# Sums over a 64-step chunk: one 128-row product per head pair, or two 64-row products on two row tiles, with new issue orders around them

## The reference, cut to what matters

```python
alpha = jax.nn.sigmoid(jax.nn.silu(x @ Wad.T + bad) @ Wau.T + bau)
alpha = jnp.clip(alpha, ALPHA_MIN, 1.0)
...
def chunk_step(S, inp):
    qc, kc, vc, ac, bc = inp
    O_inter = jnp.einsum('bcd,bde->bce', qc, S)
    cl = jnp.cumsum(jnp.log(jnp.maximum(ac, 1e-07)), axis=1)
    cum = jnp.exp(cl[:, :, None, :] - cl[:, None, :, :]) * mask[None, :, :, None]
    A = jnp.einsum('bid,bijd,bjd->bij', qc, cum, kc * bc)
    O = O_inter + jnp.einsum('bij,bje->bie', A, vc)
```

## Time and profile before

| what | us |
|---|---|
| median of 3 runs (2667.97 to 2676.7) | 2672.06 |
| the profiled execution, its own time | 2680.18 |
| its span, first to last instruction | 2677.7 |
| stage three | about 960 to 2678 of the span |
| a round: from 977.4 (first F of lane a) to 2593.6 (last of lane b) lie 15 rounds and the 39.7 from lane a to b | 105.1 |
| PE busy over the span | 2339.2 (87%) |
| ACT, DVE busy | 1622.6 (61%), 1615.5 (60%) |
| granted TensorE clock, mean; from 1100 to 2600 | 0.974; 1.00 |

### The profile page before, as it was taken

How to read it: one execution, slowest core, us unless ns; L and a number is a source line. 1 busy time by engine, 2 the same in 40 slices (tenths; PEclk the granted TensorE clock), 3 DMA queues, 4 the chain that set the end, 5 groups by cost and what they waited for, 6 DMA issues and landing times.

```text
span 2677.7 us, 93035 instructions
## 1 busy us (share of the span) xinstructions
PE 2339.2 (87%) x41378; PEld 1733.9 (65%) x41378; DVE 1615.5 (60%) x3692; ACT 1622.6 (61%) x3788; POOL 295.4 (11%) x396
## 2 busy tenths in 40 slices
PE   3888888888888559999999999999999999999997
PEld 2666566666666337767667677676676676776765
DVE  3666766676667555655665655555555656565564
ACT  2767666766676335656656656656566566566663
POOL 0001110111010001011001001100110011011100
PEclk8999999999999779999999999999999999999998
DMA  3000000000000100000000000000000000000000
GB/s 110 8 9 7 10 8 9 9 8 8 9 9 8 31 25 7 6 8 7 7 9 7 7 8 7 7 7 6 9 7 7 9 6 7 8 7 6 8 6 4
DMA packets 55338, 29.76 MB, mean 11 GB/s; under 512 B 24225, under 2 KB 53217, under 8 KB 54945
## 3 DMA queue, kind: packets, MB, share of 16 engines
q1 hardware_dynamic: 50624, 21.90, 3.0%
q10 hardware_dynamic: 4320, 1.97, 0.3%
HBM read 18.60 MB, written 5.24 MB: 9 GB/s over the span
## 4 chain that ended last, share of the span: by engine, by line
PE 38%; DVE 13%; ACT 11%; issue 2%; DMA 0%; SPq 0%; DVEq 0%
PE bank L1120 5%; PE bank L1187 2%; PE bank L1317 2%; ACT PT L1372 2%; DVE h L1520 2%; DVE zels L451 2%; ACT zels L1372 2%; DVE m L449 2%; PE bank L1250 2%; PE bank L1150 1%; PE bank L356 1%; PE bank L1310 1%; DVE h L1633 1%; PE bank L1160 1%; ACT zels L1392 1%
## 5 line engine op out<-in xcount | busy, mean ns | idle before, releaser
L1030 POOL TENSOR_TENSOR PT<-zels,unit 128x512 f32<-128x512 f32 x160 | 203.7, 1273 | 1469.5 <-ACT zels L1372 1282.0
L356 PE MATMUL bank<-w_gate,ident 128*128 128x128 f32 (+3 forms) x1024 | 316.0, 397 | 14.4 <-DVE mx L876 14.4
L425 ACT ACTIVATE zels<-zels 128x512 f32<-128x512 f32 x384 | 237.8, 632 | 105.4 <-DVE zels L451 105.0
L451 DVE TENSOR_TENSOR zels<-bank,m 128x512 f32<-128x512 f32 x384 | 265.6, 692 | 13.3
L449 DVE TENSOR_REDUCE m<-bank 128x4 f32<-128x512 f32 x384 | 262.1, 683 | 18.2 <-PE bank L370 10.4
L391 PE MATMUL bank<-ident,zels 128*128 128x128 f32 x1536 | 223.0, 282 | 17.7 <-ACT zels L425 13.2
L1372 ACT ACTIVATE zels<-bank 128x512 f32<-128x512 f32 (+1 forms) x256 | 142.6, 573 | 151.8 <-PE bank L1219 76.1
L391 PEld LDWEIGHTS bank<-ident,zels 128*128 128x128 f32 x1536 | 170.9, 143 | 54.8 <-ACT zels L425 38.6
L1372 ACT ACTIVATE PT<-bank 128x512 f32<-128x512 f32 x256 | 148.0, 598 | 92.5 <-PE bank L1293 50.4
L428 ACT ACTIVATE PT<-bank 128x512 f32<-128x512 f32 x384 | 202.3, 597 | 2.4 <-PE bank L391 2.3
L356 PEld LDWEIGHTS bank<-w_gate,ident 128*128 128x128 f32 x1024 | 159.8, 194 | 57.6 <-issue 33.7
(11 more groups left out here) (292 smaller groups left out, 5025.2 us busy)
## 6 DMA issues: line engine op xcount, KB each, us to landing
ctxT<-in_ctxT_dram SPq DMA_DIRECT2D x64, 48.0 KB, 1.8
x_after_cross_attention<-x SPq DMA_DIRECT2D x32, 64.0 KB, 1.5
h<-x_after_cross_attention SPq DMA_DIRECT2D x8, 256.0 KB, 2.8
xin<-x_after_cross_attention SPq DMA_DIRECT2D x32, 64.0 KB, 1.8
out_dram<-xn SPq DMA_DIRECT2D x32, 64.0 KB, 1.6
x<-in_xT_dram ACTq DMA_DIRECT2D x30, 64.0 KB, 1.8
input_integers<-xq SPq DMA_DIRECT2D x8, 128.0 KB, 2.0
xq<-input_integers SPq DMA_DIRECT2D x32, 32.0 KB, 1.8
```

The lines of the kernel that those rows point to most:

```text
L356: mm(bank[:, 0:cols], ident[:, :], w_gate[:, :, :].rearrange("p a b -> p (a b)")[:, 0:cols], start=True, stop=True)
L425: act.activation(n.zels[:, u, :], n.zels[:, u, :], ACT.Exp, scale=ATT_SCALE).then_inc(ph.act[s], ph.AC.step(s, f"{t}P{u}"))
L451: dve.tensor_tensor(n.zels[:, u, :].rearrange("p (h k) -> p h k", h=HU), scores, top.unsqueeze(2).broadcast_to([P, HU, P]), ALU.subtract). ...
L1030: pool.tensor_tensor(n.TI[:, k % 2, :, :], (n.PT0, n.PT1)[k % 2][:, :, 1, :], unit[:, :].unsqueeze(1).broadcast_to([P, NP, DK]), ALU.add)\
```

## The change

Stage F now takes two products for a pair: chunk 0 with rows 0 to 63 of the logarithms as weights and the upper left 64x64 block of `since` as the moving operand, chunk 1 with rows 64 to 127 and the lower right block. The first goes to bank 2, the second to bank 3. There are 16 products of 64 rows and 64 moving columns in place of 8 of 128 and 128. One semaphore step `cum` after the last product replaces `cum0` and `cum1`. ScalarE still takes four exponentials of 128x512; each now reads one chunk's bank and writes 64 of every 128 columns. The four order strings are new, and so is the fill: 13 units for each lane in both, at other stages. POOL's string starts lane b at stage 44 rather than 18.

```diff
-            "pe": (35, "100101001010001101011011010111010101000110010000101101110101110011101010110100110101",
...
+            "pe": (35, "100100100110101001010101100110010110001001101100101101110110110011101010110110010110",
...
-            "pool": (18, "111101101011001001110111000110001001101110010101110001000101010011110110101101000100",
...
+            "pool": (44, "000001101010101001110010111111010101010110001001000110111111000000000101101101011100",
...
-        CWARM = {"h": 0, "conv": 2, "alpha": 3, "F": 0, "norm1": 0, "bc": 0, "fc": 4, "pj": 0, "yq": 1, "Wo1": 0,
-                 "lna": 1, "lnav": 0, "lngv": 1, "lny": 0, "lnyv": 0, "lnf": 0, "lnfv": 1,
+        CWARM = {"h": 1, "conv": 0, "alpha": 0, "F": 1, "norm1": 0, "bc": 3, "fc": 0, "pj": 0, "yq": 3, "Wo1": 0,
+                 "lna": 0, "lnav": 1, "lngv": 0, "lny": 0, "lnyv": 0, "lnf": 3, "lnfv": 1,
...
                         for i in range(2):
                             act_did(f"aL{i}")
                             for p in range(4 * i, 4 * i + 4):
-                                last = mm(pair_out(p, 2), n.B[:, p, :], since[:, :], start=True, stop=True)
-                            last.then_inc(pc.pe[s], pc.PE.step(s, f"cum{i}"))
+                                for c, (lo, hi) in enumerate(halves):
+                                    last = mm(b[2 + c][:, p * DK:(p + 1) * DK], n.B[lo:hi, p, :], since[lo:hi, lo:hi], start=True, stop=True)
+                        last.then_inc(pc.pe[s], pc.PE.step(s, "cum"))
...
                         for i in range(2):
-                            pe_did(f"cum{i}")
-                            f(quad(n.Fp, i), b[2 + i][:, :], ACT.Exp, f"Fp{i}", scale=-1.0)
-                            f(quad(n.Fm, i), b[2 + i][:, :], ACT.Exp, f"Fm{i}")
+                            chunk = slice(DK * i, DK * (i + 1))
+                            sums = b[2 + i][:, :].rearrange("p (a t) -> p a t", t=DK)
+                            pe_did("cum")
+                            f(n.Fp[:, :, chunk], sums, ACT.Exp, f"Fp{i}", scale=-1.0)
+                            f(n.Fm[:, :, chunk], sums, ACT.Exp, f"Fm{i}")
```

More of the change, by code:

```diff
@@ L498, in decoder @@
         pc = Part(sem, "c",
-            [*norm_pe("a"), "mid", "al0", "al1", "gb", "cum0", "cum1", "Q0", "Q1", "K0", "K1", "ssq", "V1", "M", "cdT", "cds", "V0",
+            [*norm_pe("a"), "mid", "al0", "al1", "gb", "cum", "Q0", "Q1", "K0", "K1", "ssq", "V1", "M", "cdT", "cds", "V0",
              "T0", *[x for name in SOLVE for x in ((name, "KmT") if name == f"W{LEVELS - 2}" else (name,))], "S", "Oi", "O0", "O1", "mo", "bc", y_pe[0], "Wo1", "lngv",
@@ L998, in decoder @@
         CSLOTS = slots_of(CSTAGES, {
-            "pe": (35, "100101001010001101011011010111010101000110010000101101110101110011101010110100110101",
[L1000 to L1004, removed]
-            "pool": (18, "111101101011001001110111000110001001101110010101110001000101010011110110101101000100",
-                   "10011100110011100100010001100000110101"),
+            "pe": (35, "100100100110101001010101100110010110001001101100101101110110110011101010110110010110",
+                   "11010101010110100101000111000100101000"),
+            "act": (35, "001010011001010101000111010110010001101110001100101110111011011001011101011010011011",
+                   "01101001110001100110101010000001001100"),
+            "dve": (36, "010000101110010010110000111101010010010111001010111011010110011110101001101100111010",
+                   "10101011000011101010011100010000010101"),
+            "pool": (44, "000001101010101001110010111111010101010110001001000110111111000000000101101101011100",
+                   "10100100101011101101000101110110010011"),
         }, TAILS)
         C_LOADS = 4
-        CWARM = {"h": 0, "conv": 2, "alpha": 3, "F": 0, "norm1": 0, "bc": 0, "fc": 4, "pj": 0, "yq": 1, "Wo1": 0,
-                 "lna": 1, "lnav": 0, "lngv": 1, "lny": 0, "lnyv": 0, "lnf": 0, "lnfv": 1,
+        CWARM = {"h": 1, "conv": 0, "alpha": 0, "F": 1, "norm1": 0, "bc": 3, "fc": 0, "pj": 0, "yq": 3, "Wo1": 0,
+                 "lna": 0, "lnav": 1, "lngv": 0, "lny": 0, "lnyv": 0, "lnf": 3, "lnfv": 1,
                  "y": {"S": 0, "P": 0, "OT": 0, "AT": 0}}
```

## The result

The changed kernel takes 2753.3 us (median of 4 runs, 2741.4 to 2758.8), the kernel before beside it 2670.1 us: a ratio of 1.030, 95% interval 1.027 to 1.033. It is slower by 83 us, and outside the range. The profiled execution took 2741.4 us, the least of the four, with a span of 2739.0 against 2677.7.

The account below looks back on a forecast made before the run. TensorE's order was taken to set the pace, with 7.8 us idle in a 105.1 us round. Products, step and fill at 0, orders -1 us and a shorter last record -1 took 2672.06 to 2670 us; range 2640 to 2699.

Parts of the forecast that it names:

- Part 1: F's products on PE: 16 overlapping pairs take 1.8 us, as 16 records before, since weight loads set the pace; 0.
- a shorter last record: F's last record on PE was said to be shorter, taking 1 us more off the total time.
- Part 2: One step for both banks: exponentials start 1.0 us later but are covered; cost 0, up to 0.3 a lane.
- Part 3: Fill on PE: 13 units a lane before and after, 0.21 us each; sum unchanged, worth something only inside a wait.
- the walk: Hand trace of one round, 1641.37 to 1746.51, under the new orders; 22 waits, good to about 1 us a round.
- Part 4: The new orders: leads and lags at eight places sum to -0.05 us a round, -1 us over 16 rounds.
- leads at `S` and in `O`: Lane b's `S` starts 0.6 us ahead, and the end of `O` comes 0.8 us ahead, in the new order.
- The clock: TensorE's granted clock was forecast to stay at 1.00 from 1200 to 2500 us.
- The slower rival: Lane b's norm behind lane a's convolution delays `yq`; 2688 us, told by over 2.5 us before L1334; 0.26 with small waits.
- the rule of the Trainium skill: Up to 2x for F's products, as the halved-F rival: 14 to 29 us less, 2643 to 2657 us; chance 0.10.

Follow-up runs that it names:

- before, new fill: The kernel before with only the changed kernel's table of fill, orders and gate sums as before; 2712.2 us, ratio 1.014.
- before, less fill: The kernel before with 6 of its 26 units of fill a round taken away; 2674.5 us, ratio 1.001.
- new orders, old F: The changed kernel's order strings and fill with the kernel before's whole products and two steps; 2733.7 us, ratio 1.018.
- after, fill behind: The changed kernel with 10 more units of fill a round, ahead of F and so behind the waits; 2773.3 us, ratio 1.037.
- after, old fill: The changed kernel with the fill table of the kernel before; 2784.1 us, ratio 1.043.
- after, norm first: The changed kernel with lane b's output projection and norm turns ahead of lane a's convolution on VectorE and ScalarE; 2848.9 us, ratio 1.067.
- before, one stretch new: The kernel before with the changed kernel's turns from lane a's first norm to its gate sums, on three engines; 2779.1 us, ratio 1.040.
- after, stretch back: The changed kernel with the kernel before's fill and its turns from lane a's first norm to its gate sums; 2763.7 us, ratio 1.035.
- gate sums alone: The kernel before with only the new F lines; first run 2683.7 and 2692.2 us (two other executions disturbed), second run 2685.9 us, ratio 1.006.
- one step alone: The kernel before with the gate sums' two semaphore steps made one, products whole; 2680.3 us, ratio 1.003.
- the waits filled: The changed kernel with lane b fill added, 6 units before the query (L1334), 4 before the convolution's second half (L1148); 2708.1 us, ratio 1.012.

## Why the prediction was wrong

The sum of what was measured, from 2753.3 us down: filling two waits takes away 45 us (the clock), halving the fill, from 36 units to 18 that stand in waits, takes away 24, the old gate sums change nothing that can be told (+3.7), and 13 are left to the new turns (2683.9 and 2687.6 against 2670.6 and 2674.9 beside them). The shares go by this order of steps: taken away first, the old gate sums gave some 20 us, with the scatter told above.

- **Part 1** was right: nothing won, nothing lost in the products' time (1.93 us from F's first product to the next stage's in the changed kernel at full clock, against 2.09 and 1.98 before). The 1 us taken off for a shorter last record isn't there: it is 272 ns long and was 275. What it left out is the clock: in the old orders a wait before the 64-row products is followed by falls, and the same wait before whole ones is not.
- **Part 2** was mis-sized at its edge. Cost 0 was taken; measured in the old orders was a wait of 0.28 us a round, near the end of the bound (0.3), and in the new ones nothing.
- **Part 3 is the step that failed first.** "The sum is unchanged" counts the units and not their places. The same 13 units moved alone cost 39 us. The 5 units ahead of `conv` and `alpha` covered waits, as the walk itself says of lane b, where it has 0.8 and 1.2 us come out instead of 0.1, but the price of fill where it had been hiding a wait was not carried through both lanes.
- **Part 4** found the places of the waits, and nearly their sizes: 1.26 before L1334 (1.55 forecast), 1.0 (1.2) and 0.5 (0.8) for lane b's `alpha` and `conv`, 0.8 (0.85) before L1183, 0.5 (0.65) for `fc`, and the six that were to go went. It came out level, though, where the measured round is 2.0 us longer at full clock, and PE idle for 1.5 us more. A part of the miss is a wait that it did not have, 0.7 us before L1133. Another may be the round that it was held against, one of 105.1 us, where undisturbed rounds of the same trace take 103.84: the round walked has a wait of 0.8 us before L1234 that they lack. How much of the 1.2 us between them the walk carried into the new order can't be told, so this share stays open.
- The **leads at `S` and in `O`** (0.6 and 0.8 us) were priced as if PE set the pace there. In the old orders a wait of 0.7 us removed before L1293 was worth 0.15 us, and 1.28 us of fill 0.23.
- **The clock is the largest miss, 45 us.** The text has 1.00 from 1200 to 2500; it was 0.98, with 68 us at half. The slower rival had the right wait, the right cause (lane b's norm behind lane a's convolution) and the right consequence ("a lower clock behind it"), but put its point at 2.5 us and priced no fall. The wait was 1.26 us, half of that, and was followed by a fall in 6 of 15 rounds. Nothing in the trace of before excluded it: its three falls stand behind waits of 0.9, 1.9 and 1.6 us (the last two for nothing that the profile names), which a reading by a window of 1300 us at clock 1.00 does not show.

On the rule of the Trainium skill ("TensorEngine Tiling (Array Packing)", section "Theoretical Speedup"), up to 2x for a dimension up to 64: the trace shows no gain over whole products, since 762 records of 64x64 take the 50.9 us of 400 whole ones. What the two row tiles give is that the 64-row records overlap: 32 of them take 2.00 us, where one after another at 0.116 us each they would take 3.7, an estimate from the earlier trace rows. The prediction read the rule as a gain from splitting a whole product, which is not what these rows show. The Trainium skill, "TensorE: Matmul & The Clock Gate", section "LDWEIGHTS (loading the stationary operand)", says that a load's time goes by its columns and not by the contraction; the trace agrees: with half the rows and still 128 columns, a load takes 199 ns, and took 191.

What stays open is why one wait of a given length is followed by a fall and another is not (below), and which of the new turns make the 13 us at full clock. No run changed GpSimd's order by itself.

## What to carry to other kernels

Where an engine is busy for 93% and its waits are short, what counts is not how many waits a new order removes but which long ones it makes, what stands in them and what behind them. Put a price on a fall of the clock behind each of TensorE's longest waits (45 us here, for two waits of 1.3 and 1.0 us a round), and put filler work into those waits first. Cost filler by its place and its lane, never by the sum of its units. And take the baseline of a walk from the rounds that are undisturbed (here 103.84 us, where the mean is 105.0).

## What the runs showed of the hardware

In a stage where TensorE is busy for over 90% of the time, its granted clock falls from 2.4 to 1.2 GHz soon after idle waits of 0.6 to 2.7 us, and not after each wait of a given length. In this table a fall counts for a wait if it begins within the wait or within 8 us of its end. All of them begin by 2.9 us after the end; those before L370 in "before, less fill" begin 0.0 to 0.3 us after it. The table is worked out from the waits and the clock records of each trace; it has the waits of this length from 1010 us to the end of the last round.

| kernel | wait of PE | times | followed by a fall |
|---|---|---|---|
| all | 0.7 us, before L409 | 15 each | 0 |
| before, new fill | 0.7, before L1148, lane a (0.7 and 0.8 shortly ahead) | 15 | 4 |
| before, new fill | 1.0, before L1148, lane b | 12 | 0 |
| before | 1.1, before L370 | 15 | 0 |
| before, less fill | 1.1, before L370 | 15 | 4 |
| new orders, old F | 1.3, before L1333 | 15 | 12 |
| after | 1.3, before L1334 | 15 | 6 |
| after | 1.0, before L1148, lane b | 14 | 2 |
| after, fill behind | 1.3, before L1334 | 15 | 11 |
| after, old fill | 1.9, before L1334 | 15 | 8 |
| after, norm first | 2.7, before L1148, lane a | 15 | 15 |
| after, norm first | 1.0, before L1148, lane b | 13 | 10 |
| before, one stretch new | 1.9, before L1333 | 15 | 9 |
| before, one stretch new | 2.2, before L391 | 15 | 2 |
| after, stretch back | 1.1, before L1161 (64-row products) | 15 | 15 |
| gate sums alone, first and second run | 0.6, before L1161 (64-row products) | 15 each | 3, 5 |
| before; one step alone | 0.6, before L1160 (whole products) | 15 each | 0 |

Length alone does not decide. What PE does behind the wait has a hand in it: the last two rows have the same wait. The same wait in the same kernel is followed by a fall in some rounds and not in others. A stretch at half clock lasts 3.4 to 13.7 us in the changed kernel. Its 68 us cost 33 in the profiled execution (spans of 2739.0 against 2706.3 with the waits filled), half of the time, as a clock at half speed would have it; the median of its runs, 12 us above that execution, lost more.

Two row tiles do work side by side on 64-row weights: 32 such records take 2.00 us, and 16 whole ones 2.02 to 2.05.
